# Cross attention of layer 0: the products that subtract the row maxima on 32-row tiles, four issued together behind the scores of both halves of the queries

## The reference, cut to what matters

```python
x = x + _L0_xattn_ref(_layernorm(x, axis=-1), ctx, ctx, mask, Wq, bq, Wk, bk, Wv, bv, Wo, bo)
# within it, for each head:
#   p = softmax over the keys of (Q @ K^T / sqrt(64))   masked keys are taken care of by replaced keys and a bias
#   out = p @ V, heads joined, @ Wo + bo
```

## Time and profile before

| | |
|---|---|
| median of 3 runs | 5889.34 us (5887.56 to 5891.16) |
| the profiled execution | 5890.79 us, its span 5889.0 us |
| PE, share of the span | 5275.3 us, 90% |
| POOL | 2217.9 us, 38%, nearly all of it in this block |
| ACT, DVE | 3176.3 us, 2752.2 us |
| this block's scores | from 435 to 2530 us of the span |
| exponentials, line 2434 | 816 of 1.11 us |
| additions, lines 2580 and 2589 | 400 each of 2.37 us |
| line 2326 | 1632 products of 64x128 by 64x512, bf16 |

### The profile page before, as it was taken

One profiled execution on the slowest core, in us unless ns is written; L12 is line 12 of the kernel. 1 busy time (PEld: TensorE's weight loads), 2 busy tenths in 40 slices (PEclk: granted clock), 3 DMA queues, 4 the chain that ended last, 5 costly groups with the idle time before them and its releaser, 6 DMA issues. The chain is left out here.

```text
span 5889.0 us, 69174 instructions
## 1 busy us (share of the span) xinstructions
PE 5275.3 (90%) x27886; PEld 1716.5 (29%) x27886; DVE 2752.2 (47%) x3206; ACT 3176.3 (54%) x3203; POOL 2217.9 (38%) x1113
## 2 busy tenths in 40 slices
PE   6869999999999999988989689999886788888889
PEld 2213333333333333333244311111342111111123
DVE  6664455454545453014541410000246999988723
ACT  3355545555555555521022389999224677777861
POOL 1108898989898899924634000000000000000000
PEclk7859999999999999999999799999896799999999
DMA  1000000000000000000000120000203000000010
GB/s 50 15 0 1 1 1 1 1 1 1 1 1 1 1 1 1 1 20 22 2 0 4 39 96 10 20 11 2 77 27 118 18 11 11 11 11 11 7 45 31
DMA packets 64432, 100.75 MB, mean 17 GB/s; under 512 B 9846, under 2 KB 49880, under 8 KB 62000
## 3 DMA queue, kind: packets, MB, share of 16 engines
q1 hardware_dynamic: 63906, 95.50, 4.8%
q10 hardware_dynamic: 206, 0.83, 0.0%
HBM read 70.85 MB, written 25.31 MB: 16 GB/s over the span
## 5 line engine op out<-in xcount | busy, mean ns | idle before, releaser
L2434 ACT ACTIVATE Pr<-ps,key_bias 128x1024 f32<-128x1024 f32 x816 | 892.8, 1114 | 1015.4 <-PE ps L2326 1013.4
L2522 DVE TENSOR_REDUCE red<-ps 128x2 f32<-128x1024 f32 (+1 forms) x767 | 907.6, 1185 | 959.8 <-PE ps L2311 954.5
L2580 POOL TENSOR_TENSOR Ps<-Ps,Pr 128x1024 f32<-128x1024 f32 x400 | 946.0, 2365 | 215.9 <-ACT Pr L2434 215.9
L2589 POOL TENSOR_TENSOR Ps<-Ps,Pr 128x1024 f32<-128x1024 f32 x400 | 947.7, 2369 | 0.0
L3207 DVE TENSOR_REDUCE red<-ps 128x1 f32<-128x512 f32 (+3 forms) x1024 | 877.4, 907 | 95.7 <-PE ps L3080 76.0
L3163 ACT ACTIVATE Pr<-ps 128x1024 f32<-128x1024 f32 x816 | 786.2, 1021 | 228.2 <-PE ps L3090 227.3
L2324 PE MATMUL ps<-Q,Kr 64*128 64x512 f32 x3264 | 841.9, 594 | 0.5 <-DVE red L2522 0.2
L2343 PE MATMUL ps<-Pr,Vc 128*64 128x512 f32 x3264 | 790.0, 605 | 0.0
L3337 ACT ACTIVATE Pr<-ps 128x2048 f32<-128x2048 f32 x467 | 726.5, 2029 | 3.4 <-PE ps L3300 3.3
L3080 PE MATMUL ps<-Kp,Q 52*128 52x512 bf16 (+1 forms) x1664 | 442.6, 412 | 170.6 <-DVE red L3207 124.9
L3103 PE MATMUL ps<-Pr,V 128*9 128x512 f32 x3264 | 436.1, 606 | 0.0
(11 more groups left out here) (578 smaller groups left out, 5219.0 us busy)
## 6 DMA issues: line engine op xcount, KB each, us to landing
L_dram_K<-parts SPq DMA_DIRECT2D x26, 384.0 KB, 3.2
Kp<-L_dram_K SPq DMA_DIRECT2D x14, 624.0 KB
L_dram_K<-parts SPq DMA_DIRECT2D x26, 256.0 KB, 2.9
wB<-L_ffn_shares SPq DMA_DIRECT2D x1, 6144.0 KB
w<-L_ffn_experts_w_dram SPq DMA_DIRECT2D x24, 256.0 KB
Kp<-L_dram_K SPq DMA_DIRECT2D x14, 416.0 KB
wB<-L_ffn_shares SPq DMA_DIRECT2D x1, 3584.0 KB, 12.7
ctx<-ctx_dram SPq DMA_DIRECT2D x13, 256.0 KB, 7.5
```

The lines of the kernel that those rows point to most:

```text
L2434: nc.scalar.activation(Pr[:, t % 4, half].rearrange("p a n -> p (a n)"), ps[:, 2 * half:2 * half + 2, :].rearrange("p a n -> p (a n)"), AC ...
L2522: nc.vector.tensor_reduce(red[:, g // C % 2, q, :, g % C], ps[:, maxima_bank(g, s, steps, q):maxima_bank(g, s, steps, q) + 2, 0:ctx.keys_i ...
L2580: nc.gpsimd.tensor_tensor(into, into, src, ALU.add).then_inc(*summed0.up())
L2589: nc.gpsimd.tensor_tensor(into, into, src, ALU.add).then_inc(*summed1.up())
```

## The change

The products of line 2326 are cut from 64 to 32 rows. `mz` is filled so that a head's first 32 rows hold the maxima of half 0 and its other 32 rows those of half 1; the other half's columns are zero there. `scores` for half 0 now issues only the two score products; `scores` for half 1 issues its two and then all four subtracting products, one after the other. The signal `scored` for half 0 thus comes with them. On DVE lines 2563 and 2565 become two instructions each, one for each half of the queries.

```diff
             for a in range(2):
                 nc.tensor.matmul(ps[:, 2 * half + a, :], lhsT=Kr[head(a), j % 16, s * 128:(s + 1) * 128], rhs=Q[head(a), p % 3, sl], start=True, stop=False)
-            for a in range(2):
-                mm = nc.tensor.matmul(ps[:, 2 * half + a, :], lhsT=ones[head(a), :], rhs=Qa[head(a), p % 2, sl], start=False, stop=True)
-            mm.then_inc(*scored.up())
+            if half == 0:
+                return
+            for h, both in enumerate(HALVES):
+                for a in range(2):
+                    at = slice(64 * a + 32 * h, 64 * a + 32 * h + 32)
+                    mm = nc.tensor.matmul(ps[:, 2 * h + a, :], lhsT=ones[at, :], rhs=Qa[at, p % 2, both], start=False, stop=True)
+                mm.then_inc(*scored.up())
...
-                nc.vector.tensor_reduce(mz[:, :, :, 0], red[:, p % 2], AX, ALU.max, negate=True).then_inc(*rows_step.up())
+                for h in range(2):
+                    of_half = slice(4 * h, 4 * h + 4)
+                    last = nc.vector.tensor_reduce(mz[:, of_half, :, 32 * h], red[:, p % 2, of_half], AX, ALU.max, negate=True)
+                last.then_inc(*rows_step.up())
                 nc.vector.wait_ge(*rows_step.at(3 * p + 2))
-                nc.vector.tensor_tensor(mz[:, :, :, 1], neg[:], mz[:, :, :, 0], ALU.subtract).then_inc(*rows_step.up())
+                for h in range(2):
+                    of_half = slice(4 * h, 4 * h + 4)
+                    last = nc.vector.tensor_tensor(mz[:, of_half, :, 32 * h + 1], neg[:, of_half], mz[:, of_half, :, 32 * h], ALU.subtract)
+                last.then_inc(*rows_step.up())
```

## The result

| | before | after |
|---|---|---|
| median | 5889.42 us (9 runs, 5883.63 to 5895.52) | 5908.7 us (9 runs, 5900.72 to 5915.73) |
| ratio | | 1.0031, 95% interval 1.0021 to 1.0041 |
| profiled execution, span | 5890.79 us, 5889.0 us | 5914.79 us, 5913.0 us |

The change made the kernel slower by 19 us, 0.3%. The forecast was 5896.5, called no change, the range 5878 to 5917; the rival of the second subtraction held up behind POOL stood at 5910. The 19 us are more than the 11.8 that the forecast still counted as no change. The profiled execution of the changed kernel is one of its long ones. Its runs lie 15 us apart, those of before 12.

The account below looks back on a forecast made before the run. The PE was taken to set the pace, POOL only in the last 51 tiles. -9.5 (shapes) + 0 + 6.7 (exponential) + 0.95 (POOL's last run) + 9.1 (DVE) = +7 on 5889.34: 5896.5 us, range 5878 to 5917.

Parts of the forecast that it names:

- the rival of the second subtraction held up behind POOL: Line 2565's second half on DVE waits for a whole POOL addition: 2.31 x 6 = 13.9 more, 5910; chance 0.28.
- The bound: PE sets the pace while tiles share it with maxima (354 tiles); POOL does in the last 51 tiles.
- Four at once, and the shapes: Ordinary tile on the PE: four products save 0.20, two shape changes cost 0.20; 4.55 stays; 95 other tiles -0.10.
- the unknown way from 32 rows to 64: PE's return from 32-row to 64-row tiles, not in the trace: bounds 0 and 0.15, taken as 0.10.
- The later exponential: Half 0's exponential 0.95 later: `rows` +0.47, three-tile chunk's last tile +0.94, next scores' 0.3 wait covered; +6.7 in all.
- the special tiles: 24 tiles counted apart: `rows` +0.47, three-tile chunk's last +0.94, `output` +0.95, first of a turn +0.57, six each.
- ACT's copies with a cover of 0.1: Copies at s = 0 end 0.1 ahead of the next maxima; just enough, except 7 tiles losing their 0.10 gain.
- DVE against POOL: POOL's run 0.95 later delays DVE's line 2565 and 2538: keys +0.57, `output` +0.95, six times each, +9.1.
- the step that put the second half of line 2565 at 0: On DVE, the second instruction follows the first ahead of POOL's next addition: 0 taken, bounds 0 and 2.31.
- the prediction's own sign: Wrong if an ordinary tile isn't within 0.05 of 4.55, or a turn isn't between 1 shorter and 4 us longer.

Follow-up runs that it names:

- the first experiment: The changed kernel with DVE making each mz column for both halves in one instruction; 5896.64 us, ratio 1.0014.
- the last experiment: The changed kernel, one DVE instruction per mz column, subtraction behind the next maxima's reduction, second maxima ahead of the subtracting products in ordinary tiles; 5874.15 us, ratio 0.9976.
- the shape alone: The changed kernel with its 32-row products issued two by two, each pair behind its own half's scores; 6080.91 us, ratio 1.0323.
- The order alone: The kernel before with its 64-row subtracting products moved behind both halves' scores, no DVE split; 5903.85 us, ratio 1.0025.
- The split alone: The kernel before with only DVE's lines 2563 and 2565 in two instructions each, old layout; 5889.42 us, ratio 1.0005.
- four instructions: The changed kernel with the DVE subtraction in four instructions instead of two; 5920.44 us, ratio 1.0062.

## Why the prediction was right, and where it was off

- **The bound.** Right. The PE sets the pace of the turns: what the tiles' steps on it gain or lose is what they gain or lose, in the first and the last experiment too. In the last 51 tiles it is POOL: the PE's step there went from 4.217 to 4.112, and yet the stretch from the last `rows` to the end of the last `output` takes 265.4, where it took 265.0.
- **Four at once, and the shapes.** Right to 0.01: 4.557 for 4.55, with keys and values -0.10. The value taken for the unknown way from 32 rows to 64, 0.10, is what the shape alone measured.
- **The later exponential.** Right: +0.49 for +0.47, +0.96 and back 0.3 for +0.94 and 0.3. The order alone shows that this, and not the new shape, makes the special tiles longer.
- **ACT's copies with a cover of 0.1.** Right: tiles with keys and values are 6.503 and don't wait longer, and the cover is gone only around the three-tile chunk, where the tile with `queries` loses 0.09.
- **DVE against POOL.** Right where one instruction is caught: `output` +0.95 for +0.95, the first tile of a turn 7.20 in the first experiment for 6.606 + 0.57 = 7.18.
- **The forecast itself.** Its 7 us are near what the first experiment measured, 8.6 (5896.64 against 5888.02). What failed is the step that put the second half of line 2565 at 0. I took it because there is a gap between two additions; the gap is there, but the second instruction did not get through it in three turns of six in the profiled execution. The rival had the mechanism, and 13.9 for six caught turns; measured are 12.7 for three. Its price of 2.31 a turn left out that the gap on the PE, 2.92, lowers the clock. With three caught turns at 3.8 to 5.1 each it comes to 5909.
- **Luck.** That 5908.7 stands so near to the rival's 5910 is luck: half as many caught turns at nearly twice the price. The time lies in the range only because the range was drawn to take in this rival; no change, as forecast, it was not, and the chances (0.49 slower, 0.40 same) had leaned the other way than the forecast itself. By the prediction's own sign, a turn at most 4 us longer, it was wrong in three turns of the five.

The Trainium skill, "SBUF — State Buffer", section "SBUF: two separate sides", says that the shared ports are held for the whole instruction and the loser blocks fully. The trace agrees: the first subtraction of 16 elements takes 2.26, up to the end of the addition under way, and the caught pair 4.47.

Still open is what decides between slipping in and being caught. The split alone was caught in none of those turns, the shape alone in none either, and the changed kernel in three, with starts of the second instruction and of POOL's next addition in all of them within about 0.02 of each other. The spread of the changed kernel's runs, 5900.7 to 5915.7, would fit one to five caught turns an execution. Only one execution has a profile, and the kernel before spreads by 12 with none caught, so this was not shown.

## What to carry to other kernels

Count the changes of tile shape along the PE's order before cutting products to fewer rows: each costs 0.1 us here, half of what four bf16 products at once gave, so such products belong next to work that changes the shape anyway. When a step is moved, ask also where it moves the run of an engine that shares something with another: here POOL's 0.95 put its additions over DVE's two-input instructions. And don't split such an instruction in two beside a long POOL instruction, however small the parts are: it did no harm in two of the kernels here, but cost 3.8 to 5.1 us each time the second part was caught in the changed one. Put it where nobody waits behind it.

## What the runs showed of the hardware

- A change of tile shape on the PE costs 0.09 to 0.11 us in every direction seen, 32 rows to 64 included. From 32 rows to float32 scores on 64 it costs 0.1 more (scores of 1.06 between two 32-row groups, 0.95 with such a group only behind them, 0.86 among their like): their second weight load starts 0.11 behind the products' start there, and with it in the kernel before, and the first products last 0.69 instead of 0.59.
- Four bf16 products on 32-row tiles into four PSUM banks run in one slot: 0.32 to the next shape, as long as a single pair with its change.
- Between two of POOL's additions of 2.35 us at most two tiny two-input DVE instructions passed, 0.1 apart. Ahead of the last maxima the second of two passed in three cases of six in the changed kernel and in six of six in both the split alone and the shape alone. With four instructions the third never passed with the first two: it waited 2.3 us in all six.
- Behind eight of the nine gaps of 2.9 to 3.0 us on the PE (three in the changed kernel, six with four instructions) the granted clock was at the 1.2 GHz level for a stretch; behind the ninth, and behind all those of 0.6 to 1.7 in these turns, it stayed at 2.4 GHz. This made a wait of 2.2 us cost 3.8 to 5.1.
